# A two-layer model on one core: routing one step earlier, attention's end one slice later, a bias moved between stages

## What is computed

```
x = x + attention(xn) + ffn(xn)
attention: q, k, v = xn @ W + b; softmax over the 8 sequences at each position and head
           out = (softmax(q k / sqrt(8)) v) @ out_w.T + out_b
ffn:       sum over experts e of  combine[t,e] * (silu(xn @ w1_e.T) * (xn @ w3_e.T)) @ w2_e.T
           + a shared expert of the same form
combine:   s = sigmoid(xn @ w_gate.T); 16 experts in 4 groups of 4; the two groups whose two
           best scores add up highest; the four best scores in these; weights w / (sum w + 1e-6)
```

## Time and profile before

| engine | busy us | share of span | instructions |
|---|---|---|---|
| TensorE (PE) | 306.7 | 85% | 1771 |
| VectorE (DVE) | 314.0 | 87% | 826 |
| ScalarE (ACT) | 178.7 | 50% | 499 |
| GpSimd (POOL) | 250.5 | 70% | 162 |

### The profile page before, as it was taken

The page is one execution under the profiler, slowest core; times in us unless marked ns, Lnnn a source line. Parts: engine busy times, 40 slices in busy tenths (PEclk is TensorE's granted clock), DMA queues, the critical chain, the costliest instruction groups (busy, mean ns, idle before and its releaser), DMA issues. The chain is left out here.

```text
span 360.1 us, 5666 instructions
## 1 busy us (share of the span) xinstructions
PE 306.7 (85%) x1771; PEld 252.2 (70%) x1771; DVE 314.0 (87%) x826; ACT 178.7 (50%) x499; POOL 250.5 (70%) x162
## 2 busy tenths in 40 slices
PE   0568876889898887588989999999989989999895
PEld 0346665767686666477868887887879878798675
DVE  5995899989878777976999999899998999989795
ACT  3345755878777667676241623425325253252520
POOL 4184577836657482214989889879898798987771
PEclk9987999999999999979999999999999999999999
DMA  5690000000000000004953424313443334253201
GB/s 139 168 295 1 2 0 1 2 2 0 3 0 3 0 0 3 0 5 121 175 130 98 110 83 104 101 63 121 116 96 100 109 106 99 69 136 97 49 2 58
DMA packets 21321, 24.91 MB, mean 69 GB/s; under 512 B 2420, under 2 KB 12060, under 8 KB 21292
## 3 DMA queue, kind: packets, MB, share of 16 engines
q1 hardware_dynamic: 20248, 24.09, 25.4%
q10 hardware_dynamic: 820, 0.39, 0.4%
q0 software_dynamic: 224, 0.08, 0.1%
HBM read 22.19 MB, written 2.36 MB: 68 GB/s over the span
## 5 line engine op out<-in xcount | busy, mean ns | idle before, releaser
L885 POOL TENSOR_TENSOR prod_pv<-prob,qkv 128x1024 f32<-128x1024 f32 x32 | 69.6, 2196 | 16.9 <-DVE att L1589 15.1
L875 POOL TENSOR_TENSOR prod_qk<-qkv 128x1024 f32<-128x1024 f32 x32 | 76.7, 2413 | 4.6 <-DVE above L1459 4.6
L773 ACT ACTIVATE Q<-Q 128x512 f32<-128x512 f32 x48 | 27.3, 582 | 47.2 <-PE Q L942 47.2
L942 PE MATMUL Q<-bias,ones 128*128 128x400 f32 (+1 forms) x64 | 30.7, 480 | 15.9 <-ACT v_ext L663 7.0
L1575 DVE TENSOR_REDUCE scr<-prod_qk 128x128 f32<-128x1024 f32 x32 | 38.8, 1213 | 5.4 <-POOL prod_qk L875 5.4
L1630 DVE TENSOR_TENSOR hid<-T,sgc 128x512 f32<-128x512 f32 x64 | 43.4, 677 | 0.1
L942 PEld LDWEIGHTS Q<-w,hid 128*128 128x128 f32 x288 | 37.5, 191 | 3.6 <-DVE hid L1630 0.7
L942 PEld LDWEIGHTS VN<-w,hid 128*128 128x128 f32 x288 | 37.7, 191 | 3.0
L942 PE MATMUL Q<-w,hid 128*128 128x128 f32 x288 | 38.0, 275 | 0.5 <-DVE hid L1630 0.5
L1589 DVE TENSOR_REDUCE att<-prod_pv 128x128 f32<-128x1024 f32 x32 | 38.2, 1194 | 0.0
L942 PE MATMUL VN<-w,hid 128*128 128x128 f32 x288 | 37.9, 274 | 0.0
(11 more groups left out here) (186 smaller groups left out, 809.5 us busy)
## 6 DMA issues: line engine op xcount, KB each, us to landing
cw<-comb_table SPq DMA_DIRECT2D x62, 256.0 KB, 4.7
out_x<-fin SPq DMA_DIRECT2D x7, 256.0 KB, 4.6
x<-in_x SPq DMA_DIRECT2D x2, 256.0 KB, 3.0
wraw<-in_w1T SPq DMA_DIRECT2D x1, 512.0 KB, 4.0
w3raw<-in_w3T SPq DMA_DIRECT2D x1, 512.0 KB, 4.7
w<-in_w2T SPq DMA_DIRECT2D x1, 512.0 KB, 5.7
cw<-comb_table SPq DMA_DIRECT2D x4, 128.0 KB, 3.4
rope_s<-in_c_sin ACTq DMA_DIRECT2D x1, 256.0 KB, 5.0
```

Source lines behind the costliest of these rows:

```text
L773: act.activation(gated[:, :], gate_bank(n, s)[:, :], ACT.Silu).then_inc(sg_ready, 1)
L875: pool.tensor_tensor(prod_qk[:, t % 2], bc(qkv2[:, TH * half + t, j, 0:D], 1, NB), qkv2[:, :, j, D:2 * D], ALU.mult).then_inc(qk_prod, 1)
L885: pool.tensor_tensor(prod_pv[:, t % 2].rearrange("p (h e) b -> p b h e", e=HD), bc(prob[:, t].rearrange("p h b -> p b h"), 3, HD), qkv2[:, ...
L942: return pe.matmul(o, lhsT, rhs, start=start, stop=stop)
```

## The change

Nothing of what is computed changes. Four things move.

- Routing, first half: scores in step 8 instead of 9 (`sigmoid(0)` further ahead in ScalarE's step, and the dummy square root that loads the square root's table again, too); pairs and group maxima at the end of step 8; comparison, counts and mask inside step 9; top four and half of the marks at its end; the other half in step 10, weights at its end; sums and weights in step 11. The two fills of `above` and `wsel` get a place and a semaphore of their own (`route_cleared`). `sc`, `pairs` and `gs` leave the region that is used twice, since they are now written while stage one's arrays are live.
- Attention's end: the exponential at p = 2 instead of 1 (behind that slice's Silu), the transposes and `attT` at 9 instead of 8, the product at 12 instead of 11, the residual at 14 instead of 13. The last attention keeps its places.
- `sum_of_p` and `over_sum` at p = 5 and 6 instead of 2 and 3 (the last attention keeps them).
- `biased` leaves stage one's steps: chunks 0 and 1 ahead of the first `prod_qk`, chunks 2 to 7 in slots 0 to 5, between `prod_qk` 0 and `less_max`. The residual waits for the four biases of its half.

More of the change, by code:

```diff
@@ L116, in build @@
         bout2 = sb("bout2", [P, D])
+        gs = sb("gs", [P, NH * NG])
+        pairs = sb("pairs", [P, NH * NG, NPAIR])
+        sc = sb("sc", [P, NT, NE])
         rope_c = sba("rope_c", [P, NJ, 2, D])
@@ L288, in build @@
         early.close()
-        sc = sb("sc", [P, NT, NE])
-        pairs = sb("pairs", [P, NH * NG, NPAIR])
-        gs = sb("gs", [P, NH * NG])
         above = sb("above", [P, NH, NG, NG])
@@ L317, in build @@
         r_sig = sem("r_sig")
+        r_cleared = sem("r_cleared")
         r_step = sem("r_step")
@@ L1442, in route_pairs @@
                 step_of(V.tensor_tensor(pairs[:, :, 5:6], s4[:, :, 0:1], s4[:, :, 3:4], ALU.add))
+            def route_cleared():
+                V.memset(wsel[:, :, NE:NE + 1], ROUTE_EPS)
+                V.memset(above[:, :, :, :], 0.5 - TOPG).then_inc(r_cleared, 1)
             def route_groups(h):
                 routed()
-                if h == 0:
-                    V.memset(above[:, :, :, :], 0.5 - TOPG)
-                    V.memset(wsel[:, :, NE:NE + 1], ROUTE_EPS)
                 step_of(V.tensor_reduce(gs[:, :], pairs[:, :, :], AX_X, ALU.max))
@@ L1454, in route_above @@
                 routed()
+                if h == 0:
+                    dve.wait_ge(r_cleared, 1)
                 gv = gs[:, :].rearrange("p (t g) -> p t g", g=NG)
```

## The result

The changed kernel took 357.36 us (median of six runs, 354.49 to 357.7) against 361.4 us, a ratio of 0.9873 [0.9838, 0.9908]. The forecast was 356.3. The profiled execution took 357.43 us, its span is 355.6, so 4.5 us of span are gone. Where, is best read in stretches that begin and end at the same instruction: a step goes from one `RECIPROCAL root<-root` of VectorE to the next, stage two from the first `hid` to the last `fin`.

The account below looks back on a forecast made before the run. In stage two TensorE and VectorE are nearly always busy; order can give back VectorE's idle time. Stage one -1.4 and stage two -4.15 make -5.55 from 361.89: 356.3 us, own range 354.8 to 358.2, wider range 353.6 to 360.0.

Parts of the forecast that it names:

- The bias in stage one: Stage one: without GpSimd's bias holding back `root<-ss`, 0.42 us gained a step in four steps, -1.7 us.
- Both blocks: Steps 8 and 9: VectorE's pairs and mask each wait out a GpSimd addition; 0.8 us lost, against 0.3 gained without.
- the one on step 9: Step 9: the mask waits for GpSimd's addition, so `den` comes some 0.6 us later; +0.6 us.
- Steps 10 and 11: Step 10: mask, top-8 and half of the matches leave the path; -0.5 us, bounds 0 and 1.2.
- The Silu waits: Stage two: VectorE's `sgc` waits for ScalarE's Silu go, except part in the last slot; 3.65 us gained.
- The Silu after it has one slice more: Stage two: a slice of 2.65 us covers exponential and table load, 0.64 + 1.28 us, before the following Silu.
- The third-product waits: Stage two: VectorE's waits of 0.68 and 0.67 us for GpSimd's `prod_qk` go as `att` comes earlier; 1.35 us gained.
- the uncovered biases: Slots 3 and 5: GpSimd's added bias lacks full cover, costing 0.2 and 0.65 us; 0.85 lost.
- (1): Rival, stage two: Silu waits turn into `prod_qk` waits of the same slots; 359.2 us, chance 0.20.
- (2): Rival: no blocks, all of the waits go, GpSimd not late; 354.4 us, chance 0.10.
- (3): Rival, stage two: exponential so late that `prob` is 1.6 us late for `prod_pv` in seven slots; 367 us, chance 0.08.
- (4): Rival, stage two: the bias finds no cover on GpSimd, 6.4 us lost; 361.8 us, no change, chance 0.07.

Follow-up runs that it names:

- e6: e4 with biases out of slots 3 and 5: four ahead of stage two's first product, one each in slots 0, 1, 2, 4; 356.26 us.
- e9: Kernel before with the bias move and the later end of attention together, routing not moved; 354.82 us, ratio 0.9818.
- e7: Changed kernel plus seven unused TensorE products ahead of the transposes of `attn` in step 9; 354.94 us, ratio 0.9821.
- e3: Kernel before with only routing moved; 363.21 us, ratio 1.0058.
- e4: Changed kernel with counts and mask ahead of the residual's sum in step 9; 354.18 us, ratio 0.9811.
- e8: e4 with two more unread instructions like `den` ahead of `den` in step 9; 357.14 us, ratio 0.9852.
- e10: e4 with ScalarE's copy `attT` of attentions 2 and 4 two slices later, behind the next exponential; 353.75 us, ratio 0.9776.
- e1: Kernel before with only the bias moved; 361.52 us, ratio 1.0012.
- e2: Kernel before with only the exponential and attention's end moved, including its sums; 357.87 us, ratio 0.9899.

## Why the prediction was right, and where it was not

**The sum.** 357.4 against 356.3, faster as forecast and inside its own range. Step 9 missed by 1.4 us and stage two by 0.6; steps 4 to 7, step 8 and the start of the kernel gave 0.9 of that back unforeseen, 0.2 of it (the start) by chance. That the number came out within 1.1 us is in part luck.

**The bias in stage one** was right in kind and too small: 0.42 us a step were taken from TensorE's gap before its projection; 0.53 came in steps 5 to 7 (15.09 instead of 15.62), 0.60 in step 4, so nearly all of what `root<-ss` lost. The gap on TensorE was the wrong place to read it: four steps gave 2.20 us, near the upper bound of 2.4.

**Both blocks happened**, pairs 1.41 and mask 1.37 us. The Trainium skill's rule in SBUF — State Buffer, "Who interferes with whom", for two SBUF inputs beside a reading GpSimd, fits both, where the one row of before had left it open for these instructions. In e6 the pair instruction stood longer than by that rule: it began at 160.57 under one addition and stood through the next, which started at 161.58, 2.53 us in all. In step 8 the block took 0.5 of what the bias gave (e9: 14.94, after: 15.43), the forecast had 0.8.

**The step that failed is the one on step 9**: "`den` ... comes some 0.6 us later". It came 0.38 us later in its step, so the delay itself was over-estimated; yet the step grew by 1.97 us, not 0.6. What was missed is what the delay does on TensorE: its wait for `attn` grew from 1.62 to 2.00 us, and the granted clock behind it was 0.66 on average, between the levels of 2.4 and 1.2 GHz. e7 filled the wait, left the delay, and had 1.58 of 1.97 us back; the 0.39 left is the delay. The prediction read such a fall at 152 to 158, as a thing that is there, and did not ask which change of a wait would bring another.

**Steps 10 and 11** came out at -0.48 against -0.5, but not as worked out: step 10 gave 1.15 and the rest took 0.67 back. That the two add up to the forecast is luck. With routing moved (e6 with its four biases left out) the stretch takes 18.27 to 18.54 us where its mean granted clock is 0.91 (e3, e4, e8), and 18.96 to 19.01 where it is 0.82 (the changed kernel, e7, e10): 0.4 to 1.2 us gained. Without the move it takes 19.42 to 19.44 at either (e9; before, e1). Whether the clock fell in step 9 doesn't decide which: it did in e3, and did not in e7 and e10. What does is not shown.

**The Silu waits**: 3.65 forecast, 3.1 measured. In the last slot the 0.65 was right (2.48 to 1.83). The failed sentence is "The Silu after it has one slice more". In slots 3 and 5 neighbours are 8 slices apart, so `attT` of the attention before stands one slice ahead of the exponential and holds back the Silu between them; e10 shows that with this copy behind the exponential the waits are gone. The prediction priced just this in the last slot and did not look for it in the other two short distances.

**The third-product waits** went (1.35), and the uncovered biases made new ones of 0.24 and 0.69 in slots 3 and 5, forecast 0.2 and 0.65. The sizes are right and their meaning is not: 0.85 was counted as lost, but without those biases stage two is no shorter (186.69 in e2, 186.94 in e6, 186.79 in the changed kernel), since the same VectorE would then wait at `sgc` for the copy.

**The rivals.** (1) is a small part of what happened, in slots 3 and 5. (2), no blocks, fell. (3), `prob` too late for `prod_pv`, is there with 1.9 us on GpSimd, 0.9 at most, and does not reach VectorE. (4), no cover, holds only where the exponential stays in its place: 3.1 us in e1. Of the signs named beforehand, the stretched pairs, `root<-ss` at 0.17 and a stage two below 189 us are there. "No `sgc` wait over 0.3" is not: one has 0.59. Of "steps 5 to 8 at 15.2", 5 to 7 came out at 15.1 and step 8 at 15.43, for which the prediction's own sum had +0.2. And one sign of being wrong is there, `prod_pv` waiting for `prob`, though it reached no other engine. The prediction summed the parts as if independent; the cover for the biases was made by the other part.

## What to carry to other kernels

A wait that grows on TensorE may have to be priced twice: by its growth (0.4 us here), and by the clock at which the work behind it runs (1.6 us); so compare the growth with waits of the same trace behind which the clock fell or did not. A VectorE instruction with two SBUF inputs belongs where GpSimd is known to be still, ahead of the result that wakes it rather than behind. Test parts together as well as one by one: here one part alone gave nothing, and on top of another 0.8%.

## What was not expected of the chip

The clock. Behind waits of 1.62 us (before, e2, e6) and 1.63 us (e1, e4, e9, e10) for `attn` in step 9 it stayed at 1.00; behind 1.89 us (e8) it stayed so in the profiled execution, and the runs fall into two groups 2.2 us apart; with 2.00 us the profiled executions of the changed kernel and of e3 show eight products at 1.91 and 1.53 us instead of 1.05. Seven products that nothing reads, 1.54 us, kept it up (e7). In steps 10 and 11 the clock falls in every execution, its mean there between 0.76 (e2) and 0.92 (e6), and 0.91 in e4 against 0.82 in e10, whose stage one is the same. What exactly decides stays open.
